# Node work in parts beside the decay and edge passes, half-size decay slots, and constant matmuls in TensorE's pauses, in a four-layer graph network kernel

## The chip, the cores and the metric

The kernel runs on one core of a Trainium2 chip. A core has TensorE (PE: matmuls, into the accumulators PSUM, of 8 banks of 512 float32 columns), VectorE (DVE), ScalarE (ACT), GpSimd (POOL) and SyncE (SP), which here issues all DMAs, in one queue in the order of its program. The engines run apart and wait for each other by semaphores. Each engine takes its instructions in the order written. The metric is the device time of one execution in microseconds (us), lower is better.

## The reference

A graph of 3327 nodes with 64 features each, `x`, and a weighted matrix `adj` of 3327 x 3327 (44 MB in float32), so large that each use of it is a pass that streams it from HBM. Four layers, each closed by a residual and a layernorm:

```python
x = _layernorm(x + hops(x, adj, W))        # layer 0: twice tanh([adj @ x, x] @ W[k])
x = _layernorm(x + ode(x, adj))            # layer 1: 1 - 0.1 x - 0.01 sum(x * (adj @ x))
# layer 2, "decay": each node weighs its last 100 neighbours by powers of 1/2
support = x @ weight
mask = (adj != 0); rank = cumsum(mask, axis=1); deg = rank[:, -1:]
k = minimum(deg, 100.0); pos = rank - (deg - k)
w = mask * where(pos > 0, 0.5 ** (k - pos), 0.0)
x = _layernorm(x + (w @ support + bias))
# layer 3, "hyper", two iterations of _layer(x, H=adj), then x = _layernorm(x + result)
def _layer(x, H, ...):
    structural = norm(x @ W); Q = x @ Wq + bq; V = x @ Wv + bv
    edge_feat = H.T @ V                                         # pass edge
    att = softmax(Q @ edge_feat.T * scale * H, axis=1)          # pass att
    importance = 0.5 * structural + 0.5 * att.mean(axis=0)
    comp_mask = softmax(importance) >= th_comp
    xn = (x * comp_mask) / norm                                 # the normalised rows
    edge_mask = softmax((xn @ xn.T) * H, axis=1) >= th_edge     # pass cos
    H_pruned = H * edge_mask * comp_mask; node_mask = ...
    agg = (H_pruned.T * dv_isqrt) @ (x_final @ W) * de_inv      # pass down
    return relu(dv_isqrt * (H_pruned @ agg) @ Theta)            # pass up
```

## The kernel before

The matrix is padded to 3328 = 26 x 128 and taken in 26 blocks of 128 rows, 1.70 MB each. A pass streams the 26 blocks. The passes are, in order, hop0, hop1, ode, decay0, decay1, and then twice edge, att, cos, down, up (edge0 to up0, edge1 to up1). For the feature-wise passes (hop, ode, edge, down, up) TensorE makes a gather of each block: 8 float32 matmuls (16 instructions in the trace) with 64 features of a node block as stationary operand and the block as moving one; the result, features by nodes, lies in two halves of 1664 columns (13 column blocks of 128) on the two halves of the partitions.

Decay is made by columns: decay0 takes the first quarter (832 columns) of either half of each block, decay1 the second, 26 steps each. In a step VectorE makes a 0/1 mask of the half block (line 1056), TensorE counts marks by triangular matmuls into banks 0 to 3, ACT and VectorE rectify the counts to bf16 weights (lines 911 and 1077), and TensorE multiplies three bf16 parts of the support with them, into banks 4 and 5 (decay0) or 6 and 7 (decay1). GpSimd copies the three support parts of a block into a small buffer for TensorE each step (line 512). The steps run in loops of 8, with the last two outside. Half blocks land in the same eight early slots as whole blocks (four slots, and four in the arena).

Behind decay1 one chain follows: copy of the result to `agg_f`, fold (13 matmuls that turn it to nodes by features, line 551 through `fold`), VectorE's addition of x and bias (line 1096) and layernorm (1008 to 1023), turn into features (`features_round`, 52 matmuls in the trace), copy to `xt`, value projection (`to_nodes`), value bias (1185), edge0. A similar chain stands between up0 and edge1 (fold by theta, rectify in line 1316, turn, value).

In an edge pass `between(k)` puts more work behind gather k: query projection at k = 1 and 5, structural projection at 9, transposition of the normalised rows at 13, their doubling at 16 and 19. VectorE makes the normalised rows from line 1188 (which waits for the projection at 9) to line 1200 (for which k = 13 waits).

`product` serves att and cos: TensorE makes four pieces of a block's product, VectorE multiplies with the block and takes the maximum (line 1115), ACT takes exp (938); in cos VectorE also prunes the block (1256) and TensorE adds up its columns. At the end VectorE copies the column rows (1157), TensorE transposes them (line 769), VectorE computes the node softmax with two GpSimd reductions. Behind att it then writes diagonals (1231), TensorE multiplies the mask in, VectorE masks the rows (1237, 1239), cos begins. Behind cos it writes node features (1278) and down begins.

The late passes use six slots. The queue waits for a slot's last user (`block_done`). Between edge0's loads and att0's it also waits for x and stores it in HBM (line 470), and waits until that has landed. In down the last four pruned blocks are still in slots 0 to 3 and are gathered first; their slots then take further blocks.

## Time and profile before

| | us |
|---|---|
| median of 3 runs | 1884.35 |
| lowest and highest | 1883.01, 1890.79 |
| profiled execution | 1888.18 |
| its span | 1886.5 |
| TensorE busy | 1563.6 (83%) |
| VectorE busy | 1202.5 (64%) |
| ACT busy | 672.7 (36%) |

Mean DMA rate 310 GB/s over the span. The passes in the trace: decay0 and decay1 349.8 to 502.2, edge0 528.4 to 623.4, att0 to about 755, cos0 to 979, down0 and up0 986 to 1188.7, edge1 1205.9 to 1302.4, att1 to 1429.5, cos1 to 1655, down1 and up1 1662.6 to 1865.4, then the end.

### The profile page before, as it was taken

How to read it: one execution, taken by the hardware profiler on the slowest of the kernel's cores; microseconds unless marked ns; L12 is line 12 of the kernel's file. 1: busy time of each engine (PE TensorE's matmuls, PEld its weight loads, DVE VectorE, ACT ScalarE, POOL GpSimd, SP SyncE). 2: the span in 40 equal slices, each digit the busy share in tenths (PEclk: the TensorE clock that was granted, in tenths of full speed). 3: DMA queues.
4: the chain of work that ended last, by engine and by line, in shares of the span. 5: the costliest groups of instructions: out<-in, count | busy, mean ns of one | idle time of the engine just before them, and what ended most of it. 6: DMA issues, size and time to landing. Idle time of an engine off the chain costs nothing.

```text
span 1886.5 us, 23738 instructions
## 1 busy us (share of the span) xinstructions
PE 1563.6 (83%) x9649; PEld 636.0 (34%) x9670; DVE 1202.5 (64%) x1627; ACT 672.7 (36%) x481; POOL 76.5 (4%) x148
## 2 busy tenths in 40 slices
PE   6789595799799899677768799899996777787895
PEld 2244242333344333222223244443332222232452
DVE  0000202677602688899997899223886999989897
ACT  0000100233201466477760033002664777710341
POOL 0000000233100000000000000000000000000000
PEclk9999899899999999888889999999998888889998
DMA  9959399598579999155549999799993555579994
GB/s 406 426 243 427 131 417 377 178 292 290 217 291 426 390 368 376 64 210 216 215 181 398 426 415 426 299 427 425 377 372 128 186 215 216 190 318 427 425 426 169
DMA packets 60889, 584.99 MB, mean 310 GB/s; under 512 B 6144, under 2 KB 6528, under 8 KB 20608
## 3 DMA queue, kind: packets, MB, share of 16 engines
q1 hardware_dynamic: 60800, 583.71, 77.8%
q8 instruction: 67, 1.10, 0.2%
q14 instruction: 22, 0.18, 0.0%
HBM read 581.99 MB, written 1.70 MB: 309 GB/s over the span
## 4 chain that ended last, share of the span: by engine, by line
PE 47%; DVE 28%; DMA 18%; issue 3%; ACT 2%; POOL 0%; DVEq 0%; SPq 0%; POOLq 0%; ACTq 0%
PE ps L551 46%; DMA slot<-adj_t 10%; DVE pairs L1115 10%; DVE slot L1256 9%; DMA slot<-adj 7%; PE ps L829 1%; DVE slot L1298 1%; DVE slot L1284 1%; DMA x_kept<-cur 1%; ACT pairs L938 1%; DMA pairs<-adj 1%; DVE pairs L1077 0%; DVE negmax L1126 0%; DVE arena L1231 0%; DVE hats L1298 0%
## 5 line engine op out<-in xcount | busy, mean ns | idle before, releaser
L1115 DVE CUSTOM_DVE_ANT_1 pairs<-ps,slot 128x832 f32<-128x832 f32 x352 | 345.6, 1020 | 39.2 <-PE ps L551 20.8
L551 PE MATMUL ps<-hats 64*128 64x416 f32 x832 | 226.0, 651 | 96.7 <-DVE max L1115 94.8
L938 ACT ACTIVATE pairs<-pairs,negmax 128x3327 f32<-128x3327 f32 x88 | 270.1, 3070 | 90.1 <-DVE negmax L1126 90.1
L551 PE MATMUL ps<-slot,cur 128*64 128x512 f32 (+1 forms) x1152 | 218.4, 527 | 28.9 <-DVE slot L1284 20.0
L953 ACT ACTIVATE arena<-pairs,cut 128x3328 fp8e4<-128x3328 f32 x52 | 159.8, 3072 | 88.7 <-DVE cut L1249 88.7
L1256 DVE SCALAR_TENSOR_TENSOR slot<-pairs,cut,slot 128x3327 f32<-128x3327 f32 x52 | 191.1, 3675 | 0.1
L551 PE MATMUL ps<-arena 64*128 64x416 f32 x832 | 164.5, 533 | 3.5 <-DVE max L1115 3.5
L551 PE MATMUL ps<-slot,stat 128*64 128x512 f32 (+1 forms) x672 | 129.9, 538 | 43.7 <-DMA slot<-adj_t 27.9
L551 PEld LDWEIGHTS ps<-hats 64*128 64x128 f32 x832 | 76.8, 214 | 245.2 <-DVE max L1115 190.3
L996 DVE COPY pairs<-ps 128x640 f32<-128x640 f32 x5 | 4.1, 824 | 236.3 <-PE ps L551 236.3
L551 PE MATMUL ps<-pairs,hats 128*64 128x512 bf16 (+3 forms) x1016 | 148.5, 346 | 2.7 <-DVE pairs L1077 2.5
L551 PEld LDWEIGHTS ps<-slot,cur 128*64 128x64 f32 x1152 | 78.6, 139 | 165.5 <-issue 127.6
L970 ACT ACTIVATE hats<-ps 128x2048 int16<-128x2048 int16 (+1 forms) x28 | 42.1, 1554 | 237.2 <-PE ps L829 237.1
L551 PE MATMUL ps<-slot,arena 128*64 128x512 f32 (+1 forms) x656 | 118.2, 514 | 3.0 <-DVE arena L1185 2.0
L551 PE MATMUL ps<-arena,stat 128*64 128x512 f32 (+1 forms) x576 | 105.6, 515 | 16.0 <-DMA arena<-adj_t 16.0
L1284 DVE SCALAR_TENSOR_TENSOR slot<-arena,slot 128x3328 f32<-128x3328 int8 x28 | 101.5, 3625 | 20.8 <-DMA slot<-adj 20.8
L551 PE MATMUL ps<-slot,ones 128*32 128x384 f32 (+1 forms) x832 | 103.6, 597 | 9.5 <-DVE slot L1256 9.5
L551 PEld LDWEIGHTS ps<-arena 64*128 64x128 f32 x832 | 72.7, 189 | 104.2 <-DVE max L1115 71.1
L871 ACT ACTIVATE pairs<-ps 128x1024 f32<-128x1024 f32 x5 | 5.1, 1023 | 265.5 <-PE ps L551 265.5
L911 ACT ACTIVATE pairs<-ps 128x512 int16<-128x512 f32 x104 | 53.6, 517 | 108.7 <-PE ps L551 108.7
L551 PEld LDWEIGHTS ps<-slot,stat 128*64 128x64 f32 x672 | 50.8, 142 | 122.0 <-issue 93.5
L551 PEld LDWEIGHTS ps<-pairs,hats 128*64 128x64 bf16 (+1 forms) x1032 | 58.8, 105 | 92.9 <-issue 35.8
(170 smaller groups left out, 1547.7 us busy)
## 6 DMA issues: line engine op xcount, KB each, us to landing
slot<-adj SPq DMA_DIRECT2D x173, 1664.0 KB, 9.1
slot<-adj_t SPq DMA_DIRECT2D x70, 1664.0 KB, 15.8
arena<-adj_t SPq DMA_DIRECT2D x28, 1664.0 KB, 22.6
pairs<-adj SPq DMA_DIRECT2D x19, 1664.0 KB, 12.4
slot<-adj_t SPq DMA_DIRECT2D x26, 832.0 KB, 5.0
arena<-adj_t SPq DMA_DIRECT2D x26, 832.0 KB, 5.0
hats<-adj SPq DMA_DIRECT2D x8, 1664.0 KB, 14.8
hats<-adj_t SPq DMA_DIRECT2D x8, 1664.0 KB, 14.0
```

Source lines behind the costliest of these rows:

```text
L551: return pe.matmul(o, l, r, start=start, stop=stop, skip_group_check=True)
L829: last = pe.transpose(ps[:, 4 * BANK + q * D:4 * BANK + (q + 1) * D].bitcast(BF16), sign_pairs[:, q * HALF + pair * P:q * HALF + (pair + 1 ...
L871: act.activation(agg_f[:, 0:2 * BANK], ps[:, 0:2 * BANK], ACT.Copy).then_inc(evac_act, 1)
L911: act.activation(dst, bank(c, w), ACT.Relu).then_inc(relu_act, 1)
L938: act.activation(bufs[b][:, 0:N], bufs[b][:, 0:N], ACT.Exp, bias=negmax[:, b:b + 1], accum_out=rowsum[:, b:b + 1]).then_inc(exp_done, 1)
L953: act.activation(interleaved(sign_marks[:, k * NP:(k + 1) * NP]), halves(prod[k % 2][:, 0:NP]), ACT.Sign, bias=cut[:, k % 2:k % 2 + 1], sc ...
L970: act.activation(turned[pair % 2][:, cols], ps[:, 4 * BANK:4 * BANK + HALF].bitcast(I16)[:, cols], ACT.Copy)\
L996: dve.tensor_copy(agg_f[:, 2 * BANK:HALF], ps[:, 2 * BANK:HALF]).then_inc(evac_dve, 1)
L1115: dve.tensor_tensor_reduce(out=pieces3(bufs[k % len(bufs)], c), in0=pieces_psum(piece_place(name, k, c)[0]), in1=pieces3(slot_of(name, k), ...
L1256: dve.scalar_tensor_tensor(out=slot[:, 0:N], in0=prod[k % 2][:, 0:N], scalar=cut[:, k % 2:k % 2 + 1], in1=slot[:, 0:N], op0=ALU.is_ge, op1 ...
L1284: dve.scalar_tensor_tensor(out=slot, in0=interleaved(signs[:, row * NP:(row + 1) * NP]), scalar=0.0, in1=slot, op0=ALU.is_le, op1=ALU.mult ...
L1298: dve.scalar_tensor_tensor(out=slot, in0=interleaved(turned[k // 2 % 2].bitcast(I8))[:, k % 2], scalar=0.0, in1=slot, op0=ALU.is_le, op1=A ...
```

## The change

Six edits, all at seams between passes.

1. Half-size slots. The four arena slots are split into eight half slots for decay. Slots 0 to 3 are free after ode, and edge0's first four blocks are loaded into them in the middle of decay1 (behind half 12 in the queue).
2. Decay is written out, 2 x 26 steps without loop, with all waits against constants. TensorE reads the support directly; GpSimd's copies are gone.
3. Node work in parts. The 13 column blocks form three chunks (4, 4 and 5). Fold, layernorm, turn, copy and value run by chunk with semaphores of their own (`part_*`, `agg_cols`). Chunk 0 lies wholly in decay0's quarter and runs within decay1; chunks 1 and 2 run within the first gathers of edge0. Edge gathers take the rows in the order of the chunks (`EDGE_ORDER`) and each waits for its chunk's value alone.
4. Between up0 and edge1 and at the end of the program the chain runs by chunk too, the output is stored in three parts.
5. In edge, `between` moves: query from k = 1 and 5 to 9 and 11, projection from 9 to 13, normalised rows from 13 to 16, doubling from 16 and 19 to 18 and 21.
6. `keep_running`: TensorE runs 6 matmuls of constants (zeros times ones, 512 columns, into bank 4) before it waits for the column rows, and 18 (att) or 4 (cos) behind the transposes.

```diff
+CHUNKS = [slice(0, 4), slice(4, 8), slice(8, HB)]
+EDGE_ORDER = [h * HB + b for c in CHUNKS for h in range(2) for b in range(HB)[c]]
...
+        half_slots = [early_slots[RING + i // 2][:, i % 2 * HALF:(i % 2 + 1) * HALF] for i in range(EARLY_RING)]
...
+            def decay_stream(q, ks):
+                for k in ks:
+                    n = q * NB + k
+                    free = last_early_use(RING + n // 2) if n < EARLY_RING else BASE["decay0"] + n - EARLY_RING
+                    sp.wait_ge(block_done, EARLY_RING + free + 1)
+                    dst, loaded, _ = place_of(f"decay{q}", k)
+                    src = halves(adj_t[(NB - 1 - k) * P:(NB - k) * P, :])[:, :, q * QUART:(q + 1) * QUART]
+                    sp.dma_start(halves(dst), src).then_inc(loaded, 16)
...
-            stream("decay0", adj_t, 0)
-            stream("decay1", adj_t, 1)
+            decay_stream(0, range(NB))
+            decay_stream(1, range(HB))
+
+            late_stream("edge0", adj, last=RING)
+            decay_stream(1, range(HB, NB))
...
-            sp.wait_ge(out_ready, 1)
-            sp.dma_start(out, blocks3(cur[:, :])[:, :, :]).then_inc(stored, 16)
+            for c in range(3):
+                sp.wait_ge(out_ready, c + 1)
+                sp.dma_start(out.rearrange("p (h b) d -> p h b d", h=2)[:, :, CHUNKS[c]], of_part(cur[:, :], c))\
+                    .then_inc(stored, 16)
...
-            feed_decay(0)
-            feed_decay(1)
...
+            def fold_part(c, right, ready, value):
+
+                pe.wait_ge(ready, value)
+                for b in range(HB)[CHUNKS[c]]:
+                    last = mm(ps[:, 4 * BANK + b * P:4 * BANK + (b + 1) * P], agg_f[:, b * P:(b + 1) * P], right)
+                last.then_inc(part_folded, 1)
...
+            def value_part(it, c):
+
+                pe.wait_ge(part_xt, 3 * it + c + 1)
+                for b in range(HB)[CHUNKS[c]]:
+                    last = mm(ps[:, 4 * BANK + b * P:4 * BANK + (b + 1) * P], xt[:, b * P:(b + 1) * P], W["value_w"])
+                last.then_inc(part_value, 1)
...
+                for k in range(NB):
+                    step(k, last_block=k == NB - 1)
+                    if q == 1 and k == 3:
+                        fold_part(0, ident, agg_cols[0], 1)
+                    elif q == 1 and k == 10:
+                        turn_part(0, 0, cur)
+                    elif q == 1 and k == 12:
+                        value_part(0, 0)
+
+            def keep_running(steps):
+
+                for _ in range(steps):
+                    mm(bank(4), zeros_b[:, :], ones_b[:, :])
...
+                keep_running(6)
                 pe.wait_ge(colsum_sbuf, g + 1)
...
+                keep_running(18 if sums else 4)
...
+                if it == 1:
+                    for c in range(3):
+                        fold_part(c, W["theta"], agg_cols[c], 1 if c == 2 else 2)
+                    turn_part(1, 0, cur)
+                    turn_part(1, 1, cur)
+                    value_part(1, 0)
+                    turn_part(1, 2, cur)
+                    value_part(1, 1)
...
+                    elif k == 0:
+                        fold_part(1, ident, agg_cols[1], 1)
+                        fold_part(2, ident, agg_cols[1], 1)
+                    elif k == 2:
+                        turn_part(0, 1, cur)
+                        turn_part(0, 2, cur)
+                    elif k == 4:
+                        value_part(0, 1)
+                        value_part(0, 2)
...
-                    elif k == 9:
+                    elif k == 13:
 
                         pe.wait_ge(query_f32, 2 * it + 2)
                         to_nodes(xt, W["hyper_w"], 4).then_inc(proj_psum, 1)
-                    elif k == 13:
+                    elif k == 16:
...
                 for k in range(NB):
+                    pe.wait_ge(value_ready, 3 * it + EDGE_CHUNK[k] + 1)
                     gather(f"edge{it}", k, scr_a, landed(pe, f"edge{it}", k, 0))
...
+                    if q == 1 and k == 4:
+                        decayed_part(0)
+                    elif q == 1 and k == 6:
+                        var_part(0, 0)
+                    elif q == 1 and k == 8:
+                        new_x_part(0)
+                    elif q == 1 and k == 14:
+                        value_part(0, 0)
```

How the order moves. TensorE at the seam between decay1 and edge0, before: `pairs` and `hats` are decay's weights and support copy, `cst,pairs` is the fold, `cst,cur` the turn, `wt,arena` the value projection, `slot,arena` a gather.

```order
L551 MATMUL ps<-pairs,hats 64x320 [waits relu_dve,relu_act]
L551 MATMUL ps<-pairs,hats 64x320 x5
L551 MATMUL ps<-cst,pairs 128x128 [waits evac_dve,evac_act]
L551 MATMUL ps<-cst,pairs 128x128 x12
L551 MATMUL ps<-cst,cur 64x128 [waits x_ready]
L551 MATMUL ps<-cst,cur 64x128 x25
L551 MATMUL ps<-wt,arena 128x128 [waits xt_dve,xt_act]
L551 MATMUL ps<-wt,arena 128x128 x12
L551 MATMUL ps<-slot,arena 64x512 [waits slot_loaded0,value_ready]
```

And TensorE at the same seam in the changed kernel:

```order
L587 MATMUL ps<-pairs,arena 64x320 [waits relu_dve,relu_act]
L587 MATMUL ps<-pairs,arena 64x320 x5
L587 MATMUL ps<-slot,arena 64x512 [waits slot_loaded2,value_ready]
L587 MATMUL ps<-slot,arena 64x512 x5
L587 MATMUL ps<-slot,arena 64x128 x2
L587 MATMUL ps<-cst,pairs 128x128 [waits agg_cols1]
L587 MATMUL ps<-cst,pairs 128x128 x3
L587 MATMUL ps<-cst,pairs 128x128 [waits agg_cols1]
L587 MATMUL ps<-cst,pairs 128x128 x4
```

The first gather now stands right behind decay's last matmul, and the folds of chunks 1 and 2 behind it.

TensorE in edge0 around the normalised rows (`cst,arena`), before, from the end of the projection (`wt,arena`):

```order
L551 MATMUL ps<-wt,arena 128x128 x12
L551 MATMUL ps<-slot,arena 64x512 [waits slot_loaded0]
L551 MATMUL ps<-slot,arena 64x512 x5
L551 MATMUL ps<-slot,arena 64x128 x2
L551 MATMUL ps<-slot,arena 64x512 [waits slot_loaded1]
L551 MATMUL ps<-slot,arena 64x512 x5
L551 MATMUL ps<-slot,arena 64x128 x2
L551 MATMUL ps<-slot,arena 64x512 [waits slot_loaded2]
L551 MATMUL ps<-slot,arena 64x512 x5
L551 MATMUL ps<-slot,arena 64x128 x2
L551 MATMUL ps<-slot,arena 64x512 [waits slot_loaded3]
L551 MATMUL ps<-slot,arena 64x512 x5
```

And the same place, up to the normalised rows, in the changed kernel:

```order
L587 MATMUL ps<-wt,arena 128x128 x12
L587 MATMUL ps<-pairs,arena 64x512 [waits slot_loaded5,value_ready]
L587 MATMUL ps<-pairs,arena 64x512 x5
L587 MATMUL ps<-pairs,arena 64x128 x2
L587 MATMUL ps<-slot,arena 64x512 [waits slot_loaded2,value_ready]
L587 MATMUL ps<-slot,arena 64x512 x5
L587 MATMUL ps<-slot,arena 64x128 x2
L587 MATMUL ps<-slot,arena 64x512 [waits slot_loaded3,value_ready]
L587 MATMUL ps<-slot,arena 64x512 x5
L587 MATMUL ps<-slot,arena 64x128 x2
L587 MATMUL ps<-cst,arena 64x128 [waits hat_ready,proj_read]
```

Four gathers stood between the projection and the rows; now three do.

TensorE behind attention 0 in the changed kernel (`L835` are the transposes of the column rows, `arena,ones_b` the mask product; before, the rows of `ones_b,zeros_b 128x512 x6` and `x18` were not there):

```order
L587 MATMUL ps<-ones_b,zeros_b 128x1 [waits piece_read]
L587 MATMUL ps<-ones_b,zeros_b 128x512 x6
L835 MATMUL ps<-cst,pairs 128x128 [waits colsum_sbuf]
L835 MATMUL ps<-cst,pairs 128x128 x7
L587 MATMUL ps<-ones_b,zeros_b 128x512 x18
L587 MATMUL ps<-arena,ones_b 64x512 [waits diagonal_ready]
```

The constant matmuls stand ahead of two waits of TensorE that were there before.

## Rows read from the trace of the kernel before

**Rows 1.** Stretches: length, busy of PE, PEld, DVE, ACT, POOL, PEclk, DMA share, GB/s

```profile
502.20:528.40 26.20, 10.70 (x104) 10.11 (x104) 14.31 (x15) 4.00 (x5) 0.00 (x0) 0.80 0.18 66
...
528.40:623.40 95.00, 92.16 (x526) 39.94 (x526) 12.10 (x10) 8.42 (x7) 0.00 (x0) 1.00 0.93 387
...
623.40:755.10 131.70, 123.81 (x834) 45.49 (x835) 107.91 (x289) 84.49 (x54) 0.00 (x0) 0.97 0.97 385
...
1205.90:1302.40 96.50, 93.86 (x526) 40.33 (x526) 12.10 (x10) 8.41 (x7) 0.00 (x0) 0.98 0.95 394
...
1302.40:1429.50 127.10, 122.29 (x834) 43.78 (x835) 107.63 (x288) 84.51 (x54) 0.00 (x0) 1.00 0.97 380
```

**Rows 2.** Timeline of PE in edge0: start, us, instruction, [idle before <- releaser]

```profile
565.87 11.40 PE L551 MATMUL ps<-slot,arena 128*64 128x512 f32 x64
...
578.76 3.06 PE L551 MATMUL ps<-cst,arena 128*64 128x128 f32 x52 [1.49 <-DVE arena L1200]
```

**Rows 3.** Timeline of DVE: seam behind decay, and edge0

```profile
506.56 1.89 DVE L1096 TENSOR_TENSOR arena<-ps,arena 128x1664 f32<-128x1664 f32 x1 [3.32 <-PE ps L551]
...
565.98 1.89 DVE L1188 COPY xw<-ps 128x1664 f32<-128x1664 f32 x1 [37.63 <-PE ps L551]
```

**Rows 4.** Timelines of the queue (SPq) and DVE around the two attention starts

```profile
481.66 9.07 SPq L458 DMA_DIRECT2D slot<-adj  x4
...
608.07 0.43 SPq L470 DMA_DIRECT2D x_kept<-cur  x1
...
622.41 16.79 SPq L458 DMA_DIRECT2D slot<-adj  x6
...
629.60 1.02 DVE L1115 CUSTOM_DVE_ANT_1 pairs<-ps,slot 128x832 f32<-128x832 f32 x1 [5.37 <-DMA slot<-adj]
...
1305.17 1.03 DVE L1115 CUSTOM_DVE_ANT_1 pairs<-ps,slot 128x832 f32<-128x832 f32 x1 [1.91 <-PE ps L551]
```

**Rows 5.** Stretches as in rows 1: the first gather of down0 and down1

```profile
985.90:991.70 5.80, 5.73 (x18) 2.03 (x20) 5.80 (x3) 0.00 (x0) 0.00 (x0) 0.51 0.00 0
...
1662.60:1667.90 5.30, 5.25 (x18) 1.77 (x20) 5.30 (x2) 0.00 (x0) 0.00 (x0) 0.55 0.00 0
```

**Rows 6.** Timelines of the queue (SPq) and DVE at the start of down0

```profile
991.78 5.91 SPq L458 DMA_DIRECT2D slot<-adj  x3
...
998.18 3.62 DVE L1284 SCALAR_TENSOR_TENSOR slot<-arena,slot 128x3328 f32<-128x3328 int8 x1 [4.41 <-DMA slot<-adj]
```

**Rows 7.** Timelines of DVE, POOL and PE in decay0 and decay1

```profile
411.26 0.69 DVE L1077 TENSOR_SCALAR pairs<-ps 128x512 int16<-128x512 f32 x1
...
413.09 1.02 DVE L1056 TENSOR_SCALAR pairs<-slot 128x1664 bf16<-128x1664 f32 x1
...
413.34 0.97 POOL L512 COPY hats<-arena 128x192 bf16 x1 [1.95 <-PE ps L551]
...
414.18 0.69 DVE L1077 TENSOR_SCALAR pairs<-ps 128x512 int16<-128x512 f32 x1
...
425.82 1.04 PE L551 MATMUL ps<-ones_b,hats 128*128 128x512 bf16 x4
```

**Rows 8.** Timeline of PE from up0's end to edge1's first gather

```profile
1189.84 3.17 PE L551 MATMUL ps<-wt,pairs 128*128 128x128 f32 x26 [1.12 <-ACT pairs L871]
...
1195.06 4.62 PE L551 MATMUL ps<-cst,cur 128*64 128x128 f32 x52 [2.05 <-DVE cur L1316]
...
1205.94 4.71 PE L551 MATMUL ps<-pairs,arena 128*64 128x512 f32 x16 [1.98 <-DVE arena L1185]
```

**Rows 9.** Timelines of PE and DVE between attention 0 and cosine 0

```profile
765.01 1.59 PE L551 MATMUL ps<-arena,ones_b 128*64 128x512 bf16 x4 [0.21 <-DVE arena L1231]
...
769.86 1.02 DVE L1115 CUSTOM_DVE_ANT_1 pairs<-ps,slot 128x832 f32<-128x832 f32 x1 [1.08 <-PE ps L551]
```

**Rows 10.** Timelines of DVE and the queue (SPq) at the program's end

```profile
1869.72 1.96 DVE L1316 SCALAR_TENSOR_TENSOR arena<-ps,dv 128x832 f32<-128x832 f32 x2 [3.46 <-PE ps L551]
...
1882.58 0.34 SPq L483 DMA_DIRECT2D out<-cur  x1
```

More of the change, by code:

```diff
@@ L79, in early_places @@
     for name, _ in PASSES:
[L80 removed]
+        if name.startswith("decay"):
             return places
@@ L88, in early_places, with last_early_use @@
             order.reverse()
+def last_early_use(slot):
+    order, _ = EARLY_PLACES["ode"]
+    return BASE["ode"] + max(k for k in range(NB) if order[k % EARLY_RING] == slot)
 EARLY_PLACES = early_places()
@@ L104, in late_places @@
 def late_places():
-    order, loads = EARLY_PLACES["decay1"]
-    last = {s: BASE["decay1"] + max(k for k in range(NB) if order[k % EARLY_RING] == s) for s in range(RING)}
+    last = {s: last_early_use(s) for s in range(RING)}
     last.update({s: EARLY - 1 for s in range(RING, LATE_SLOTS)})
@@ L443, in late_stream @@
                     home, _, free = LATE_PLACES[name, k]
-                    if free is None:
+                    if free is None or not first <= k < last:
                         continue
```

285 lines of the change are left out of this document (180 added, 105 removed).

## Prediction

> **What bounds the kernel now.** I read the table of stretches first: it cuts the span where one pass over the matrix ends and the next begins, and shows who is busy in each. Then the timeline of one engine at each seam, since the change works at the seams. Four things are to be seen.
>
> The seam between decay and edge0 (502.2 to 528.4) is 26.2 us in which the DMA share is 0.18 and TensorE is busy for 10.7 us [rows 1]. A fold, a layernorm on VectorE, a turn into features, the value projection and its bias run one behind the other, each over all 26 blocks. The seam from up0's end, 1188.7, to edge1's first gather at 1205.94 is 17.2 us of the same kind [rows 8].
>
> Edge0 and edge1 are bound by TensorE: busy 92.16 of 95.0 us and 93.86 of 96.5 us [rows 1]. Four gathers take 11.40 us, 2.85 each. The longest wait is 1.49 us for the normalised rows, which VectorE makes in a chain that starts at 565.98 [rows 2, 3].
>
> After edge0 VectorE's first piece of the attention comes at 629.60, 6.2 us after edge0's end at 623.4; after edge1 it comes at 1305.17, 2.8 us after its end at 1302.4. The copy of x to HBM was issued at 608.07 and the attention's first blocks only at 622.41, since the queue waits until the copy has landed, and it stood behind the last edge0 blocks [rows 4]. The two attention stretches take 131.7 and 127.1 us [rows 1].
>
> TensorE's granted clock is 0.51 and 0.55 (for the most part the 1.2 GHz level) in the first gather of both down passes, 5.8 and 5.3 us long, behind a pause for node softmax and column sums, and the DMA share there is 0.00 [rows 5]. Down's slots come free by gathers: the next block was issued at 991.78, when the first gather was done, and at 998.18 VectorE had waited 4.41 us for a block [rows 6]. There the cold gather is on the path. In the long cosine pass VectorE sets the pace, and the clock costs nothing.
>
> **The change, part by part.**
>
> *Decay.* A step takes 2.92 us (the same rectify at 411.26 and 414.18) [rows 7]. GpSimd's copy of 0.97 us in each runs a step ahead; its removal I take at nothing, bound 0 to -3 us (one wait of TensorE less, at most 0.06 us, in 52 steps). The mask starts at 413.09, before the copy at 413.34, and takes its 1.02 us whether or not a copy runs [rows 7]. The SBUF — State Buffer page of the Trainium skill ("Who interferes with whom") says that VectorE and GpSimd share a port pair as an exclusive lock and that the one that comes second blocks. The trace agrees that GpSimd comes second; were it the other way round, the removal would give up to 0.97 us a step.
>
> Into decay1 come, for chunk 0 (4 of 13 block columns): on TensorE a fold, a turn and a value part. A fold or value of 13 columns takes 3.17 us (1189.84) [rows 8], a turn 3.06 us (the same 52 matmuls at 578.76) [rows 2]: 4/13 of each is 0.97 + 0.94 + 0.98 = 2.9 us. TensorE has no room in decay, so all of it adds. On VectorE come seven wide operations of 512 elements, 1.89 x 512/1664 = 0.58 us each [rows 3], and small ones, 4.5 us in all. The largest lump (2.1 us) waits for the fold and so runs while TensorE, too, is 0.97 us behind; the rectify that it delays was done at 411.95, 1.1 us before its step began [rows 7]. I take 0, bound 2 us. Decay1 ends at 502.2 + 2.9 = 505.1.
>
> The eight half slots hold as many halves ahead as before and leave slots 0 to 3 to edge0. Edge0's first four blocks were issued at 481.66 already before the change [rows 4] and lay ready at 502, so loading them earlier gains nothing. They now stand in the queue ahead of 13 halves. A block is 1.70 MB, at 387/0.93 = 416 GB/s [rows 1] 4.1 us; four are 16 us, and the half behind them is needed 9 steps, 26 us, later. Cost 0, bound 3 us.
>
> *The seam decay to edge0.* Edge0's first gather follows the last decay matmul. What the seam held stands inside edge0: 9/13 of fold, turn and value, 2.2 + 2.1 + 2.2 = 6.5 us of TensorE. The layernorm of 18 blocks runs on VectorE beside gathers 0 to 2: a copy, then after the fold (at 4 us) some 9 us of the operations above. The last part is ready 13 us after decay's end; TensorE is there at 11 and waits 1.3 us with what it has left.
>
> *The normalised rows.* This wait grows. The projection moves from gather 9 to 13, what needs the rows from 13 to 16: three gathers lie between instead of four. From VectorE's start at 565.98 to the rows at 578.76 are 12.8 us [rows 2, 3]; three gathers cover 3 x 2.85 = 8.55, so TensorE waits 4.3 us instead of 1.49, in both iterations. Behind shorter pauses the clock was down: the gather at 1205.94, after 1.98 us, took 4.71 instead of 2.96 [rows 8], and down's first ones 5.8 instead of 3.0 [rows 5]. Lost are 1.8 to 2.8 us; I take 1.9, bound 0. The Trainium skill (TensorE: Matmul & The Clock Gate, Part 1) says that the throttled clock is the default and that activity releases it. That rule speaks against this edit and the rows agree; without it each edge pass would end 1.9 us earlier.
>
> Edge0's own work is 92.2 us [rows 1]. New end: 505.2 + 92.2 + 6.5 + 1.3 + 4.3 + 1.9 = 611.4, against 623.4: **-12.0 us**. Its sixth block is issued when gather 0 ends (508) and lands 6 us later, 20 follow at 4.1 us: the last lands near 597, before its gather at 608. So x is stored before the attention's blocks are due, and attention 0 should take 127.1 us as attention 1 does: **-4.6 us**.
>
> *The seam up0 to edge1.* TensorE folds in three parts (3.2), turns at full clock (3.06 instead of 4.62), makes value parts 0 and 1 (2.0), and waits 0.75 us for the first copy: 1188.7 + 0.75 + 3.2 + 3.06 + 2.0 = 1197.7 against 1205.94 [rows 8]; value part 2 (1.2) follows gather 0. Edge1's work is 93.86 less the 1.75 us of its cold gather, 92.1. New end 1197.7 + 1.2 + 92.1 + 4.3 + 1.9 = 1297.2, against 1302.4: **-5.2 us**.
>
> *Constant matmuls.* Four of 512 columns take 1.04 us at full clock (425.82), 0.26 each at most [rows 7]. Six are 1.6 us, mostly covered by VectorE's copy of the column rows; 18 are 4.7 us, done near 762.2, before the mask product at 763.2; four are 1.0 us, done before down's first gather. If the clock stays up, the mask's second product takes about half of its 1.59 us, and VectorE waits some 0.9 us less for the first cosine piece (1.08 us) [rows 9]: -1.7 in each iteration. Down's first gather takes 3.0 instead of 5.8 and 5.3: -2.8 and -2.4, since all behind it is bound by blocks. Together **-8.6 us**. No row shows what such a matmul does for the clock; the bounds are 0, or +2 where they run cold and delay what follows.
>
> *The end.* VectorE starts with the first fold part, 9/13 of 3.17 = 2.2 us before 1869.72; its work grows from 12.2 to 14.1 us but no longer waits for the root (0.4), so it ends 0.7 to 1 us before 1882.58, and the last part of the store is 10/26 of it, some 0.8 us less [rows 10]: **-1.8 us**.
>
> Sum: -12.0 - 4.6 - 5.2 - 8.6 - 1.8 = **-32.2 us**. The profiled execution took 1888.18 us with a span of 1886.5, 3.8 us above the median of the three runs, 1884.35. 1888.18 - 32.2 = 1856.0 for an execution like it; for the median 1884.35 - 32.2 = **1852**. Its own range is 1845 to 1859.
>
> **Rivals.**
>
> *The clock does not hold.* Behind the constant matmuls pauses of 1 to 1.5 us remain, and a pause of 1.98 us went before the cold gather at 1205.94 [rows 8]. Then the 8.6 us stay: 1861, or 1856 if one place in two holds.
>
> *Blocks become the bound in the edge passes.* Against it: 11 us of room at the last block. At 4.6 us a block the room is gone; at 4.8 each edge pass is 4 us longer: 1860.
>
> *Less is lost.* The larger wait does not lower the clock and a decay step shortens by 0.06 us: 1845.
>
> *Slower: the written-out decay stream starves TensorE.* The loop of 8 steps becomes 52 steps in straight line, 20 matmuls and their loads each. If their code came too slowly, each step would grow. It decides at 32.2/52 = 0.62 us a step; at 0.83 us (a step of 3.75) the time is 1895. Against it: decay holds 20 matmuls in 2.92 us; the turn at 578.76, written out already, has 52 in 3.06 us [rows 2]. The page Runtime: NRT & Kernel Launch of the Trainium skill ("Instruction fetch mechanics") says that fetch is sequential and mostly hidden, and that a taken branch is what breaks it; the row of the turn agrees.
>
> *It does nothing.* The seam's work collides so that edge0 ends as late as before; some part would have to wait 12 us, and nothing in the order does.
>
> **How the numbers follow.** Forecast 0.55, clock not held or in part 0.22, blocks 0.07, less lost 0.08, slower 0.04, no difference 0.04. The likeliest gives 1852; the range takes in the clock's rival and the lesser loss: 1843 to 1864. A measurement of this kernel can tell about 0.5% (9 us) from no change: faster by more 0.91, within 0.05, slower 0.04.
>
> **What would show it.** In the profile after: decay1 ends near 505 and edge0's first gather follows at once; a TensorE wait of 4.3 us for the normalised rows and a clock of 0.5 behind it; edge0 ends near 611; attention's first piece 3 us later; edge1's first gather 9 us after up0's end; clock 1.0 at the mask product and in down's first gather. I am wrong if decay steps grow, if the clock falls in spite of the constant matmuls, or if edge0 ends on a DMA wait.

## Result and profile after

The changed kernel takes 1855.36 us (median of 4 runs, 1853.72 to 1855.87), the kernel before 1885.01 us beside it: a ratio of 0.9836, 95% interval 0.9814 to 0.9859, 29.7 us faster. The forecast was 1852, 32 us faster. The two profiled executions differ by more than the medians: 1888.18 against 1855.87 us, spans of 1886.5 and 1854.1 us. Read by place, each row from the starts of the same work in both traces:

| part | from to (before) | from to (after) | change | forecast |
|---|---|---|---|---|
| start to edge0's first gather | 528.41 | 505.38 | -23.0 | -23.2 |
| edge0 | 528.41 to 624.71 | 505.38 to 612.12 | +10.4 | +11.2 |
| attention 0 | to 756.37 | to 739.41 | -4.4 | -4.6 |
| cosine 0 | to 983.60 | to 965.45 | -1.2 | -1.7 |
| down0, up0, with the pause ahead | to 1188.77 | to 1167.46 | -3.2 | -2.8 |
| seam up0 to edge1 | to 1205.94 | to 1176.52 | -8.1 | -8.2 |
| edge1 | to 1303.74 | to 1277.93 | +3.6 | +3.0 |
| attention 1, cosine 1 | to 1660.28 | to 1631.23 | -3.2 | -1.7 |
| down1, up1 | to 1865.44 | to 1833.84 | -2.6 | -2.4 |
| end | to 1886.5 | to 1854.1 | -0.8 | -1.8 |

The profile after says the same. TensorE at the seam from decay to edge0, which took 26.2 us in [rows 1] (start, us, instruction, in brackets the idle time before it): the gather stands right behind decay, the folds of chunks 1 and 2 and their turns within the gathers. The two waits left cost 0.9 us; forecast were 1.3.

```profile
505.38 2.96 PE L587 MATMUL ps<-slot,arena 128*64 128x512 f32 x16
508.27 2.27 PE L587 MATMUL ps<-cst,pairs 128*128 128x128 f32 x18
510.47 5.81 PE L587 MATMUL ps<-slot,arena 128*64 128x512 f32 x32
516.98 1.09 PE L587 MATMUL ps<-cst,cur 128*64 128x128 f32 x16 [0.70 <-DVE cur L1133]
518.26 1.31 PE L587 MATMUL ps<-cst,cur 128*64 128x128 f32 x20 [0.18 <-DVE cur L1148]
```

Edge0 and its end, of the same engine: the wait for the normalised rows, 1.49 us before [rows 2], is 4.28 us and the turn behind it takes 4.73 instead of 3.06 us, at a mean granted clock of 0.61. The last gather ends near 611, and the attention follows without a pause of the queue.

```profile
574.85 4.73 PE L587 MATMUL ps<-cst,arena 128*64 128x128 f32 x52 [4.28 <-DVE arena L1359]
...
608.03 2.96 PE L587 MATMUL ps<-slot,arena 128*64 128x512 f32 x16
612.12 0.61 PE L587 MATMUL ps<-ones_b,zeros_b 128*128 128x512 bf16 x2 [1.12 <-ACT arena L1044]
```

The seam from up0 to edge1, against 17.2 us in [rows 8]: 9.1 us from up0's end (VectorE's copy at 1167.46) to the first gather.

```profile
1168.10 3.17 PE L587 MATMUL ps<-wt,pairs 128*128 128x128 f32 x26 [0.70 <-ACT pairs L967]
1171.20 1.97 PE L587 MATMUL ps<-cst,cur 128*64 128x128 f32 x32
1173.10 1.16 PE L587 MATMUL ps<-wt,arena 128*128 128x128 f32 x8
1174.19 1.31 PE L587 MATMUL ps<-cst,cur 128*64 128x128 f32 x20
1175.43 1.16 PE L587 MATMUL ps<-wt,arena 128*128 128x128 f32 x8
1176.52 3.02 PE L587 MATMUL ps<-pairs,arena 128*64 128x512 f32 x16
```

Behind attention 0, against [rows 9]: both halves of the mask product take 0.89 us, where the second took 1.59.

```profile
740.34 4.05 PE L587 MATMUL ps<-ones_b,zeros_b 128*128 128x512 bf16 x18
746.25 0.89 PE L587 MATMUL ps<-arena,ones_b 128*64 128x512 bf16 x4 [1.86 <-DVE arena L1390]
748.05 0.89 PE L587 MATMUL ps<-arena,ones_b 128*64 128x512 bf16 x4 [0.91 <-DVE arena L1390]
```

Decay's steps are 2.92 us as before (a chunk of the rectified weights begins at 431.23, 434.15 and 437.06).

### The profile page after: what moved, and what is told of

It is laid out like the page before. It is cut to its first block, busy times and chain, and to the rows that moved or that the text cites. A ratio compares the mean times of both kernels' runs of the same rounds, so it can differ in the third digit from the quotient of the medians.

```text
span 1854.1 us, 23223 instructions
## 1 busy us (share of the span) xinstructions
PE 1579.2 (85%) x9738; PEld 640.9 (35%) x9738; DVE 1204.2 (65%) x1659; ACT 675.8 (36%) x493; POOL 28.6 (2%) x96
## 4 chain that ended last, share of the span: by engine, by line
PE 49%; DVE 30%; DMA 16%; issue 3%; ACT 2%; POOL 0%; DVEq 0%; SPq 0%; POOLq 0%; ACTq 0%
PE ps L587 47%; DVE pairs L1276 11%; DVE slot L1415 10%; DMA slot<-adj_t 10%; DMA slot<-adj 6%; PE ps L912 2%; DVE slot L1443 1%; DVE slot L1457 1%; ACT pairs L1050 1%; DVE negmax L1287 0%; DVE arena L1390 0%; DVE hats L1457 0%; ACT hats L1082 0%; DVE cur L1462 0%; DVE cut L1408 0%
## 5 line engine op out<-in xcount | busy, mean ns | idle before, releaser
L587 PE MATMUL ps<-hats 64*128 64x416 f32 x832 | 230.4, 663 | 90.2 <-DVE max L1276 87.8
L587 PE MATMUL ps<-slot,cur 128*64 128x512 f32 (+1 forms) x1152 | 213.1, 517 | 27.2 <-DVE slot L1443 19.6
L587 PE MATMUL ps<-slot,ones 128*32 128x384 f32 (+1 forms) x832 | 107.8, 617 | 7.2 <-DVE slot L1415 7.2
L587 PE MATMUL ps<-pairs,arena 128*64 128x512 bf16 (+3 forms) x800 | 107.2, 385 | 0.0
L587 PE MATMUL ps<-pairs,hats 128*128 128x512 bf16 (+1 forms) x408 | 90.3, 344 | 0.6 <-DVE pairs L1243 0.3
L1243 DVE TENSOR_SCALAR pairs<-ps 128x512 int16<-128x512 f32 x104 | 61.2, 591 | 42.7 <-PE ps L587 37.3
## 6 DMA issues: line engine op xcount, KB each, us to landing
pairs<-adj_t SPq DMA_DIRECT2D x8, 1664.0 KB, 13.8
```

The costliest lines, as they stand in the source:

```text
L587: return pe.matmul(o, l, r, start=start, stop=stop, skip_group_check=True)
L1243: dve.tensor_scalar(dst, bank(2 + c, w), 0.0, None, ALU.max).then_inc(relu_dve, 1)
```

## The experiments

Twelve kernels ran, in four groups, each group beside runs of the kernel before (medians 1885.5 to 1886.6 us). Where two variants are compared by under 2 us, their intervals overlap, and the reading rests on the traces, of which there is one execution for each kernel. How far two executions can differ where the kernels are alike shows at edge0's first gather: in seven traces of kernels that are the same up to there it starts between 503.4 and 505.8 us.

### The constant matmuls, taken out and alone

First the changed kernel without its constant matmuls:

```diff
-                keep_running(6)
...
-                keep_running(18 if sums else 4)
```

> The changed kernel without its constant matmuls (nothing else is changed). Theory: they keep TensorE's clock up at four places, which the two traces show as -1.5 us at the first cosine piece and -2.8 us at the first down block, in both iterations: without them +8 to +9 us, 1864, with a granted clock of 0.5 at the mask product and in down's first gather. Rival (the clock holds by the new rhythm of the other work, or the places are covered by something else): within 2 us of 1855.4, clock 1.0 there.

Measured: 1864.41 us (1861.77 to 1865.29), ratio 0.9876 (0.986 to 0.9893), 9.1 us slower than with them. Then the kernel before with the same two lines and their helper added and nothing else:

> The kernel before with the constant matmuls alone. Theory: -8 to -9 us against before, 1876.5, at the same four places. Rival (they act only together with the other edits, since in the kernel before the queue or VectorE is late next): less than 4 us gained.

Measured: 1877.96 us (1877.27 to 1879.62), ratio 0.9954 (0.9937 to 0.997), 8.1 us faster than before. The two agree: the constants are worth 8 to 9 us (the first comparison gives 7.5 if each kernel is set against the kernel before that ran beside it), with and without the rest of the change; the forecast had 8.6. The clock shows the mechanism. A table of stretches (length, busy of PE, PEld, DVE, ACT, POOL, PEclk, DMA share, GB/s) over the start of down0's first gathers, without the constants and then with them:

```profile
970.60:976.00 5.40, 5.36 (x14) 1.67 (x16) 5.40 (x2) 0.00 (x0) 0.00 (x0) 0.50 0.00 0
```

```profile
967.70:973.00 5.30, 5.26 (x28) 2.00 (x30) 5.30 (x2) 0.00 (x0) 0.00 (x0) 1.00 0.27 56
```

In about the same length TensorE does 14 matmuls at 1.2 GHz or 28 at 2.4 GHz. Timelines of TensorE there, without and with:

```profile
970.64 14.29 PE L587 MATMUL ps<-slot,cur 128*64 128x512 f32 x64 [1.27 <-DVE cur L1435]
```

```profile
967.74 11.39 PE L587 MATMUL ps<-slot,cur 128*64 128x512 f32 x64 [0.39 <-DVE cur L1437]
```

Four gathers lose 2.9 us, and down's blocks come later: without the constants VectorE's longest waits for a block are 6.24 us in down0 and 4.79 us in down1, where the changed kernel's are 2.28 and 2.04. By place the two traces, 9.4 us apart, do not add up as neatly: without the constants the first cosine pieces come 0.7 us later, down and up take 2.0 and 3.3 us more, and 4.1 us more are waits for single blocks in the cosine passes, whose cause no run shows; edge0 started 1.6 us earlier.

### The normalised rows one gather later

```diff
-                    elif k == 16:
+                    elif k == 17:
...
-                    elif k == 18:
+                    elif k == 19:
...
-                    elif k == 21:
+                    elif k == 22:
```

> The changed kernel with the normalised rows one gather later (behind gather 17 instead of 16, their doubling behind 19 and 22). Theory: the wait falls from 4.28 to 1.4 us and the clock stays up (turn of the rows 3.06 instead of 4.73 us), so each edge pass ends 4.5 us earlier and the kernel takes 1846.5. Rival (the pause lets blocks catch up, and the edge passes end on DMA waits when it goes): edge ends less than 2 us earlier, 1852 to 1855.

Measured: 1846.67 us (1845.76 to 1848.03), ratio 0.979 (0.9773 to 0.9806), 8.7 us faster than the changed kernel. TensorE in edge0:

```profile
572.88 3.06 PE L587 MATMUL ps<-cst,arena 128*64 128x128 f32 x52 [1.49 <-DVE arena L1359]
```

The wait is 1.49 us again, as with four gathers between in [rows 2], and the turn is at full clock. One gather more of cover, 2.85 us, takes away 2.79 us of wait and 1.67 us of clock; edge0 is 4.2 us and edge1 4.4 us shorter. This part of the change cost 8.7 us in all; the forecast had 2 x 4.7.

### The projection ahead of the queries

Here the projection (needed by the rows' chain) goes to gather 9 and the queries to 11 and 13, so that seven gathers lie between it and the rows (the expectation counts six).

```diff
                     if k == 9:
                         pe.wait_ge(value_ready, 3 * it + 3)
+                        to_nodes(xt, W["hyper_w"], 4).then_inc(proj_psum, 1)
+                    elif k == 11:
+
+                        pe.wait_ge(proj_read, it + 1)
                         on_both_partition_halves(W["query_w"], xt, 0, 4).then_inc(query_half, 1)
-                    elif k == 11:
+                    elif k == 13:
 
                         pe.wait_ge(query_f32, 2 * it + 1)
                         on_both_partition_halves(W["query_w"], xt, 1, 4).then_inc(query_half, 1)
-                    elif k == 13:
+                    elif k == 16:
```

> The changed kernel with the structural projection behind gather 9 and the two query projections behind 11 and 13, the rows behind 16 as they are: VectorE's chain of 12.8 us then has six gathers of cover. Theory: no wait and no clock loss, 4.28 + 1.67 = 5.9 us less in each edge pass; the attention 0 after it loses some 1 to 3 us of that, since the store of x lands only 4.7 us before edge0's end: 1845. Rival (blocks are the bound once TensorE does not pause): no better than the run with the rows one gather later.

Measured: 1847.89 us (1847.0 to 1848.29), ratio 0.9794 (0.9778 to 0.9811). No better than the run before it, though the wait is wholly gone. Edge0 is indeed 1.7 us shorter (100.8 against 102.5), but attention 0 takes 129.2 instead of 127.1 us. Timelines of VectorE and of the queue (SPq) at its start:

```profile
610.21 1.02 DVE L1276 CUSTOM_DVE_ANT_1 pairs<-ps,slot 128x832 f32<-128x832 f32 x1 [4.06 <-DMA slot<-adj]
```

```profile
588.58 0.43 SPq L515 DMA_DIRECT2D x_kept<-cur  x1
603.22 20.06 SPq L500 DMA_DIRECT2D slot<-adj  x7
```

x was stored behind the last edge block, and the queue waited 13.8 us for it, as in the kernel before [rows 4]. Edge1 takes 97.2 us here and 97.0 with the rows one gather later. Here three gathers of edge1 wait 1.11, 0.82 and 0.28 us for their blocks, there two wait 0.52 and 0.59 us and the turn of the rows 0.7. So 1.1 us more of waiting for blocks stand against 0.7 us less for the rows; whether blocks always come so late there, one trace cannot say.

### Constants ahead of the wait for the rows

```diff
+                        keep_running(16)
                         pe.wait_ge(hat_ready, it + 1)
```

> The changed kernel with 16 constant matmuls (of 512 columns, 0.22 us each) in both edge passes just ahead of the wait for the normalised rows, which takes 4.28 us in the changed kernel and is followed by a doubling of 4.73 us instead of 3.06 us. Theory (the larger wait costs twice: the wait itself, and 1.67 us of clock behind it): the doubling takes 3.06 us, the wait ends where it did, 2 x 1.67 = 3.3 us are saved: 1852 beside 1855.4. Rival (the constants run into the wait's end or delay the gathers): 0 to +1 us. Rival (the last blocks of the edge pass are the bound, so that a faster doubling only waits later): under 1 us, 1855.

Measured: 1854.57 us (1854.31 to 1860.13), ratio 0.9847 (0.9825 to 0.9868): not to be told from the changed kernel. The place itself behaved as expected:

```profile
569.00 3.63 PE L587 MATMUL ps<-ones_b,zeros_b 128*128 128x512 bf16 x16
573.25 3.06 PE L587 MATMUL ps<-cst,arena 128*64 128x128 f32 x52 [0.63 <-DVE arena L1360]
```

Edge0 is 1.8 us shorter and edge1 0.9. What it gained was given back behind the attentions, where nothing had been edited. The cosine stretches take 227.8 and 227.9 us instead of 226.0, and the second half of the mask product is cold (at the 1.2 GHz level) in both:

```profile
742.97 0.89 PE L587 MATMUL ps<-arena,ones_b 128*64 128x512 bf16 x4 [1.85 <-DVE arena L1391]
744.77 1.60 PE L587 MATMUL ps<-arena,ones_b 128*64 128x512 bf16 x4 [0.91 <-DVE arena L1391]
```

VectorE's first cosine piece comes 1.5 us later for it in both, which is most of the 1.8. The pauses are the same as in the changed kernel, and the clock did not hold. Over the nine kernels with 18 constants, one execution of each, the second half took 0.89 us in 14 of 18 places, 1.09 and 1.19 in two and 1.60 in these two.

### The constants' pauses filled

Built on the run before, with no pause over 0.8 us left at the mask:

```diff
-                keep_running(18 if sums else 4)
+                keep_running(25 if sums else 4)
...
+                    if h:
+                        keep_running(3)
                     pe.wait_ge(diagonal_ready, 2 * it + h + 1)
```

> The run with 16 constants ahead of the normalised rows (1854.6 us), and with 25 instead of 18 ahead of the mask product and 3 between its halves, so that no pause over 0.8 us is left there. In that run the edge passes gained 1.8 and 0.9 us, but the mask product's second half was cold in both iterations (1.60 instead of 0.89 us) and each cosine pass took 227.8 instead of 226.0 us. Theory (whether 18 constants hold the clock over the pauses of 1.85 and 0.91 us is left to chance; filled, it holds): cosine 226 us each, 1854.6 - 3.5 = 1851. Rival (the clock falls all the same, or the longer cosine passes have another cause): 1854.6.

Measured: 1855.96 us (1855.44 to 1860.5), ratio 0.9846 (0.9829 to 0.9862). Half of the theory held, that of the clock; its time did not come. All four halves are at 0.89 us:

```profile
744.28 0.89 PE L587 MATMUL ps<-arena,ones_b 128*64 128x512 bf16 x4 [0.34 <-DVE arena L1393]
746.08 0.89 PE L587 MATMUL ps<-arena,ones_b 128*64 128x512 bf16 x4 [0.16 <-DVE arena L1393]
```

Yet the cosine stretches took 226.9 and 227.9 us, and now with waits for blocks: 1.0 us in the first and 2.0 in the second, from a table of waits (us in total, times, longest):

```profile
DVE pairs L1279 <- DMA slot<-adj: 2.0, 2, 1.8
```

So a longer cosine stretch has two causes, a cold mask product and late blocks, and removing the first did not show in the time.

### The kernel before with the node work later

Only the positions in `between` as the changed kernel has them:

```diff
-                    elif k == 9:
+                    elif k == 13:
...
-                    elif k == 13:
+                    elif k == 16:
```

(and the others likewise: 1, 5 to 9, 11; 16, 19 to 18, 21.)

> The kernel before with nothing changed but the gathers behind which the first attention's node work stands: projection and queries behind gathers 9, 11, 13, 16, normalised rows behind 16, doubling 18 and 21, the distances of the changed kernel. Theory (three gathers cover too little of the chain of the normalised rows): the wait grows from 1.49 to 4.3 us and the doubling from 3.06 to 4.73 us, +4.5 us in each edge pass, less about 1 us in each that the last gathers stood waiting for blocks anyway: +7 to +9 us, 1892 to 1894 beside 1885. Rival (the wait is hidden by something in the order before, so the changed kernel's wait has another cause): 0.

Measured: 1889.09 us (1885.57 to 1893.32), ratio 1.0025 (1.0011 to 1.0039): 3.2 us slower, half of what was expected. The mechanism is there to the digit:

```profile
590.27 4.73 PE L551 MATMUL ps<-cst,arena 128*64 128x128 f32 x52 [4.28 <-DVE arena L1200]
```

Edge0 grows by 4.1 us (100.37 against 96.30) and edge1 by 3.7 (101.52 against 97.80). But attention 0 takes 127.3 instead of 131.7 us: in a longer edge0 the copy of x has landed before the attention's blocks are due. 4.1 + 3.7 - 4.4 = 3.4, which is near the 3.2 of the medians, but the traces do not prove the sum: the profiled execution of this kernel was the fastest of its seven, 2.6 us shorter than that of the kernel before, and so other places, which the edit does not touch, differ by 6.0 us the other way. What stands is that the expectation priced the wait and overlooked what a later end of edge0 gives back.

### The kernel before with x stored early

```diff
+                    if name == "edge0" and k == 5:
+
+                        sp.wait_ge(x_ready, 4)
+                        sp.dma_start(x_kept, cur[:, :]).then_inc(kept, 16)
...
-                    sp.wait_ge(x_ready, 4)
-                    sp.dma_start(x_kept, cur[:, :]).then_inc(kept, 16)
-
                     sp.wait_ge(kept, 16)
```

> The kernel before with the copy of x to HBM issued ahead of edge0's sixth block instead of behind its last. Theory (attention 0 started 6.2 us after edge0's end because the queue waited for this copy): attention's first piece comes about 3 us after edge0's end and attention 0 takes 127.1 us instead of 131.7: -4.6 us, 1880.4 beside 1885. Rival (the blocks of the attention would have been late anyway, since their slots come free by the last gathers): 0 to -2 us, 1883 to 1885.

Measured: 1881.34 us (1878.01 to 1882.69), ratio 0.9974 (0.9964 to 0.9984), 4.6 us faster; attention 0 takes 127.30 us. VectorE's first piece, at 629.60 in [rows 4]:

```profile
627.20 1.02 DVE L1116 CUSTOM_DVE_ANT_1 pairs<-ps,slot 128x832 f32<-128x832 f32 x1 [1.93 <-PE ps L552]
```

### GpSimd's copies back in decay

```diff
+            for q in range(2):
+                for k in range(NB):
+                    pool.wait_ge(decay_used, q * NB + k + 3)
+                    at = (NB - 1 - k) * 3 * D
+                    pool.tensor_copy(stat3[k % 2], support3[:, at:at + 3 * D]).then_inc(stat_ready, 1)
...
+                        if c == 0:
+                            pe.wait_ge(stat_ready, stats_before["decay"] + q * NB + k + 1)
```

> The changed kernel with GpSimd's copy of the support rows back in each of the 52 decay steps, and TensorE waiting for it, as in the kernel before. Theory (the copies ran a step ahead and cost nothing): 1855, a decay step of 2.92 us. Rival (the copies or their wait slowed the steps by up to 0.06 us): +3 us, 1858. Rival (they compete with VectorE for a port as the first to come): up to +0.97 us a step where VectorE's rectify is late, above +5 us.

Measured: 1854.28 us (1853.17 to 1856.14), ratio 0.984 (0.9823 to 0.9856). The removal of the copies is worth nothing that these runs can tell. They run every 2.92 us, beside VectorE:

```profile
432.45 1.14 POOL L578 COPY hats<-arena 128x192 bf16<-128x192 bf16 x1 [1.85 <-PE ps L594]
435.36 1.07 POOL L578 COPY hats<-arena 128x192 bf16<-128x192 bf16 x1 [1.78 <-PE ps L594]
```

### What else can be had

The projection first, and x stored ahead of edge0's block 12 (the thirteenth):

```diff
+                    if name == "edge0" and k == 12:
+
+                        sp.wait_ge(part_ready, 3)
+                        sp.dma_start(x_kept, cur[:, :]).then_inc(kept, 16)
```

> The run with the projection first (1847.9 us), and with x stored to HBM ahead of edge0's thirteenth block instead of behind its last. In that run no wait for the normalised rows was left (edge0 took 100.8 us instead of 102.5), but attention 0 took 129.2 instead of 127.1 us, with 4.06 us of VectorE's wait on a block. Theory (the queue's wait for the copy of x holds up the attention's blocks again, as in the kernel before): attention 0 takes 127.1 us, -2.1 us: 1845.8. Rival (the attention's blocks are late because edge0 is now bound by its blocks): 1847.9.

Measured: 1845.32 us (1844.63 to 1847.96), ratio 0.9785 (0.9769 to 0.9802). Attention 0 takes 127.29 us:

```profile
608.01 1.02 DVE L1277 CUSTOM_DVE_ANT_1 pairs<-ps,slot 128x832 f32<-128x832 f32 x1 [1.92 <-PE ps L588]
```

Next, whether the constants carry over to pauses that the change left alone, on the changed kernel:

```diff
             fold(1, W["w1_agg"], also=W["w1_self"]).then_inc(folded, 1)
+            pe.wait_ge(consts_made, 2)
+            for _ in range(58):
+                mm(bank(0), zeros_b[:, :], ones_b[:, :])
...
             fold(2, ident).then_inc(folded, 1)
+            for _ in range(62):
+                mm(bank(0), zeros_b[:, :], ones_b[:, :])
...
+                for _ in range(0 if q else 24):
+                    mm(bank(0), zeros_b[:, :], ones_b[:, :], start=False)
                 for c in range(2):
                     own_bits(0, c)
```

> The changed kernel with constant matmuls in three more pauses: 58 behind the fold of the second hop (a pause of 13.78 us, then four gathers in 13.65 us instead of 11.35), 62 behind the fold of the ode pass (14.99 us, then a turn of 4.88 us instead of 3.06) and 24 ahead of the first bits of decay (6.39 us, then about 1.3 us lost). Theory (a cold clock behind a pause costs the path what its rows show): -2.3 -1.8 -1.3 = -5.4 us, 1850 beside 1855.4. Rival (the ode pass is bound by its blocks, so that a faster start is waited away): -3.1, 1852. Rival (the work that saves time elsewhere makes the clock fall at another place): 0 or more.

Measured: 1854.62 us (1852.85 to 1856.48), ratio 0.983 (0.9814 to 0.9847): 0.7 us, not the 5.4 expected. Every place gave about what its row promised. The turn of the changed kernel, and the same one with constants ahead of it:

```profile
332.64 4.88 PE L587 MATMUL ps<-cst,cur 128*64 128x128 f32 x52 [14.99 <-DVE cur L1186]
```

```profile
329.99 3.06 PE L587 MATMUL ps<-cst,cur 128*64 128x128 f32 x52 [1.62 <-DVE cur L1193]
```

Edge0's first gather comes at 499.39 instead of 505.38 (the next expectation has 499.8, which is a later matmul of that gather). Against the seven traces named above, 503.4 to 505.8, the gain lies between 4 and 6.4 us. The second down pass starts 4.6 us early, and then most of it is lost: from there to the end this execution takes 224.1 us against 220.5. VectorE waits for one block of down1 2.04 us and for one of up1 1.99 us, where the stream's usual wait is 0.3 to 0.4:

```profile
1657.34 3.62 DVE L1450 SCALAR_TENSOR_TENSOR hats<-arena,hats 128x3328 f32<-128x3328 int8 x1 [2.04 <-DMA hats<-adj]
...
1824.48 3.63 DVE L1464 SCALAR_TENSOR_TENSOR slot<-hats,slot 128x3328 f32<-128x3328 int8 x1 [1.99 <-DMA slot<-adj_t]
```

The last run puts both together:

> The run with the projection first and x stored early (1845.3 us), with the constants in the three more pauses added. Those alone brought the first iteration 5.6 us forward up to the second down pass (edge0's first gather at 499.8 instead of 505.4), but the time only 0.7 us: in down 1 and up 1 two blocks came 1.7 us later than the stream's step. Theory (such late blocks are the chance of one execution, and the 5.4 us are real): 1845.3 - 5.4 = 1840, the down and up passes of the second iteration in the same time as without the constants. Rival (down and up of the second iteration end by the stream of blocks, which an earlier start does not bring forward by as much): 1844 to 1845.

Measured: 1841.83 us (1839.85 to 1845.03), ratio 0.977 (0.9754 to 0.9787), the shortest time here, 13.5 us below the changed kernel. Edge0's first gather is at 499.22, and from down1's first gather to the end its profiled execution, of 1840.29 us, takes 220.0 us: there the 5 us stay. Its five runs spread from 1839.85 to 1845.03, so the median lies between the theory's 1840 and the rival's 1844. Whether the three pauses are worth 5 us is not settled: by the medians 0.7 us once and 3.5 us once.

## Why the prediction was right, and where it was off

**Decay.** Forecast +2.9 us for three parts in decay1; measured +3.4 (505.59 for its end against 502.2). The parts are as counted (1.16 us for the fold's 8 matmuls, 1.04 for the turn, 1.16 for the value part: 3.36, not 2.9). The step that was off is the scaling by columns: 8 matmuls take 1.16 us and 26 take 3.17, which is 0.11 us each and 0.27 us once, so 4/13 of a group's duration leaves out most of that fixed part.

**The steps and the copies.** Nothing, as forecast. That written-out decay might starve TensorE fell: 2.92 us a step, and 0.57 us of waits in all in decay1.

**Edge0.** Forecast 611.4, measured near 611.0. The wait of 4.28 us, the clock behind it (1.67 us for a forecast of 1.9) and the two small waits are as the sum had them, and the run with one gather more confirms the pair. Weighed there was the rule of the Trainium skill (TensorE: Matmul & The Clock Gate, Part 1) that activity releases the throttled clock; the turn behind the wait was at 4.73 us without constants ahead of it and at 3.06 with them.

**Attention 0.** -4.4 for -4.6, for the reason given; storing x early in the kernel before gives -4.6 by itself. The reason is narrower than the forecast had it: what counts is how long before its last gather edge0's last block, and x behind it, are issued. Shorten edge0 by another 6 us and the wait is back (the projection first), lengthen the old one by 4 and it goes (the node work later).

**Seam and edge1.** -8.1 for -8.2, then +3.6 for +3.0. Together 0.7 us short. In part this agreement is luck. The forecast read 3.3 us of the gain off a low clock in the one trace it had: a turn of 4.62 instead of 3.06 us and a gather of 4.71 instead of 2.96 [rows 8]. Three runs leave this seam of the kernel before as it is. With the constants alone both were slow again; with the node work later the turn took 3.06 and the gather 4.71 us; with x stored early neither was slow, behind the same pauses:

```profile
1191.86 3.06 PE L552 MATMUL ps<-cst,cur 128*64 128x128 f32 x52 [2.05 <-DVE cur L1317]
...
1201.19 3.01 PE L552 MATMUL ps<-pairs,arena 128*64 128x512 f32 x16 [1.99 <-DVE arena L1186]
```

Seam and edge1 together take 111.6 us there and 115.0 in the profiled execution of the kernel before. The changed kernel's 110.5 is 4.5 us below the one and 1.1 below the other.

**Constants.** 8.6 forecast; 9.1 and 8.1 measured. By place, before against after: VectorE's first cosine piece comes 1.5 us earlier behind the transposes in both iterations (12.00 for 13.49 and 11.89 for 13.38 us; forecast 1.7), and down with up is 3.2 and 2.6 us shorter (forecast 2.8 and 2.4).

**The end.** Forecast -1.8, measured -0.8. The store gave its 0.8; VectorE, which was to end 0.7 to 1 us earlier, ended no earlier: from its copy at up1's end to the end of its work are 17.2 us, and 17.1 before. It did start as early as forecast. The term that failed is its work: put at 14.1 us without a wait for the root, it took 15.3 (1835.76 to 1851.02). Of that, 14.5 are its operations and 0.74 are two waits for ACT's root, of which this is the first:

```profile
1837.27 0.69 DVE L1119 TENSOR_REDUCE mean<-arena 128x8 f32<-128x512 f32 x1
...
1844.23 0.82 DVE L1119 TENSOR_REDUCE mean<-arena 128x10 f32<-128x640 f32 x1
...
1847.92 0.20 DVE L1132 RECIPROCAL var<-var 128x8 f32<-128x8 f32 x1 [0.37 <-ACT var L975]
```

Splitting the work did not take the wait for the root away, as the sum had it; it came twice instead of once (0.39 us before). The rest is the price of more operations. 512 elements take 0.69 us, not 1.89 x 512/1664 = 0.58, as the forecast scaled them in decay: from 0.69 and 1.89 follow 1.04 ns an element and 0.16 us for every operation. Seven operations in three parts pay that 14 times more, 2.2 us, where the sum at the end had 1.9 (12.2 to 14.1). So at this end the parts cost VectorE about what their earlier start gave. The Trainium skill (Perfetto Trace Analysis, Optimizing Scalar/DVE Operations) gives about 60 ns of access overhead for VectorE in SBUF and says that the profiled latency holds about twice that; 0.16 us is somewhat more than that, and its advice to form larger operations where the engine is the bound applies at this end.

**The comparison with the median.** The forecast took the profiled execution's 3.8 us above the median as something that stays. It did not: the traces differ by 32.4 us and the medians by 29.7. Where the 2.7 us between them went is not shown. One candidate is the low clock at the seam up0 to edge1, 3.3 us in this one trace and not in every execution; against it, the execution of the kernel with the constants alone had it too and was only 0.5 us above its median. Late blocks in cosine 1 are another. The table of waits of the kernel before, over cosine 1:

```profile
DVE pairs L1115 <- DMA slot<-adj: 2.7, 3, 1.3
```

The three other variants of the kernel before wait there as well, 2.7 to 4.6 us, and the ten traces of the changed kernel and its variants 0 to 2.0 us. So it looks like something that the change took away, and the sum had no term for it: it would account for the 3.2 us of attention 1 and cosine 1, where the forecast had 1.7. That, by luck, made a sum short by some 2 us in edge1, at the end and in cosine 0 look exact in the traces.

**The rivals.** The clock held in the changed kernel, in all four places; that in other variants it fell (4 of 18) shows that this rival was a real one. Blocks did not bind edge0. Edge1 has single waits of 0.3 to 1.6 us for them, and hardly gets shorter once the wait for the rows is gone (96.5 to 97.2 us in three runs, against 97.0 where 0.7 us of it are left).

**Open.** Single blocks that come some 0.8 to 1.7 us late in down, up and cosine, other ones in each execution. They are worth up to 4.6 us in one cosine pass, they blur the comparison of variants that are 2 us apart, and no run here shows their cause. Open too is how few constants would hold the clock, and which of the two places ahead of down holds it there: no run takes them out singly.

## What to carry to other kernels

A wait costs twice when the engine that waits is TensorE: here 2.8 us more of waiting brought 1.7 us lost to a lower clock behind it. So either move the producer of the awaited data ahead of work that others don't need yet (the projection before the queries), or fill the pause with matmuls of constants into a free bank, and check in the rows behind it that the clock stayed. Before splitting vector work into parts, add the fixed price of each operation and keep the waits for other engines in the sum; take a low clock that one trace shows at a seam as the chance of that execution until a second one shows it; and before pricing an edit at a seam, look at what a DMA queue is doing there: an earlier end can uncover a wait that a later one hides.

## What was not expected

- The clock behind the same pause is not the same in every execution. With 18 constants and pauses of 1.8 and 0.91 us the granted clock held in 14 of 18 places and fell wholly or in part in the others, wholly in both iterations of one kernel. The Trainium skill (TensorE: Matmul & The Clock Gate, Part 1) says that the moment of the change varies from run to run; the rows fit that, but with one execution of each kernel they do not tell a run's chance from an edit's effect. In the one kernel with these pauses filled it held in 4 of 4.
- Matmuls of zeros and ones hold the clock: down's first gathers ran at a granted clock of 1.00 with ten of them in the pause ahead (six and four), at 0.50 without.
- A gain far from the end need not arrive: some 5 to 6 us at edge0 became 0.7 us in one kernel and about 3.5 in another, with the stream of blocks at a DMA share of 1.00 through most of the last two passes.
